# A graph layer with a mixture of experts on one core: a reworked first stage, and 30 transposes of the identity on TensorE among its first transposes

## The reference

```python
# _layernorm subtracts the mean and divides by sqrt(var + 1e-5)
def gnn(H, W, bias, edge_row, edge_col, edge_val):      # H (1024, 512), 16384 edges
    HW = H @ W
    msgs = edge_val[:, None] * HW[edge_col]
    out = segment_sum(msgs, edge_row, num_segments=1024)
    return relu(out + bias)

x = x + gnn(_layernorm(x), W, bias, src, dst, edge_weight)
x = x + ffn(_layernorm(x))
# ffn: each of 1024 rows goes to the best 2 of 64 experts (512 -> 256 -> 512, silu gate),
# and to one shared expert (512 -> 32 -> 512); the experts' weights are 100 MB in float32
```

## Time and profile before

| what | value |
|---|---|
| median of 3 runs | 459.57 us (458.48 to 460.67) |
| the profiled execution | 458.82 us |
| its span in the trace | 457.1 us |
| granted TensorE clock, mean | 0.932 |
| PE busy | 391.7 us (86%) |
| VectorE (DVE) busy | 207.7 us (45%) |
| ScalarE (ACT) busy | 166.1 us (36%) |
| GpSimd (POOL) busy | 154.9 us (34%) |
| HBM read, written | 121.22 MB, 13.39 MB |

### The profile page before, as it was taken

How to read it: one execution, slowest core, us unless ns; L and a number is a source line. 1 busy time by engine, 2 the same in 40 slices (tenths; PEclk the granted TensorE clock), 3 DMA queues, 4 the chain that set the end, 5 groups by cost and what they waited for, 6 DMA issues and landing times.

```text
span 457.1 us, 6545 instructions
## 1 busy us (share of the span) xinstructions
PE 391.7 (86%) x1811; PEld 202.3 (44%) x1812; DVE 207.7 (45%) x685; ACT 166.1 (36%) x414; POOL 154.9 (34%) x262
## 2 busy tenths in 40 slices
PE   2699999999999987999999999986988979888600
PEld 1586767656565553344344443433434433343100
DVE  5889888216666586532333233313113123222036
ACT  9859999223223220233233323331213231131200
POOL 2575553014654657232333223323113122110000
PEclk9989999999999995899999999999889898898855
DMA  4999600100004545499999999999999999996068
GB/s 113 328 383 408 276 0 0 42 25 24 24 25 122 222 156 197 144 389 408 404 408 407 405 408 409 407 406 408 407 406 409 406 405 404 403 405 271 20 250 303
DMA packets 41779, 126.11 MB, mean 276 GB/s; under 512 B 7953, under 2 KB 8529, under 8 KB 41618
## 3 DMA queue, kind: packets, MB, share of 16 engines
q1 hardware_dynamic: 35954, 117.29, 66.3%
q0 software_dynamic: 5792, 8.43, 5.3%
HBM read 121.22 MB, written 13.39 MB: 294 GB/s over the span
## 4 chain that ended last, share of the span: by engine, by line
PE 81%; issue 5%; DMA 5%; DVE 3%; SPq 3%; POOL 1%; ACT 1%; ACTq 0%; DVEq 0%; POOLq 0%
PE bank L1295 29%; PE bank L1312 13%; PE bank L1168 12%; PE bank L1129 6%; PE bank L1136 6%; PE bank L1304 5%; PE bank L1288 4%; DMA w<-totals 2%; DMA X<-in_x_dram 2%; PE bank L1156 2%; PE bank L1187 1%; PE bank L1236 1%; PE bank L1177 1%; PE bank L1117 1%; SPq L398 1%
## 5 line engine op out<-in xcount | busy, mean ns | idle before, releaser
L1031 DVE SCALAR_TENSOR_TENSOR osl<-bank,b13T,osl 128x64 f32<-128x64 f32 x132 | 28.4, 277 | 171.5 <-ACT osl L675 171.5
L1295 PE MATMUL bank<-w,xhT 128*64 128x512 f32 x368 | 91.9, 645 | 14.7 <-issue 14.5
L668 ACT COPY xh<-bank 128x512 f32<-128x512 f32 x33 | 19.3, 585 | 149.0 <-PE bank L1295 149.0
L1168 PE MATMUL bank<-HW,AT 128*128 128x512 f32 x128 | 58.2, 592 | 0.0
L1295 PEld LDWEIGHTS bank<-w,xhT 128*64 128x64 f32 x368 | 28.6, 147 | 61.5 <-issue 60.1
L545 POOL DMA_INDIRECT totals<-osl,A x17 | 17.0, 1000 | 91.5 <-PE bank L1288 72.1
L1312 PE MATMUL bank<-w,osl 128*64 128x512 f32 x184 | 45.0, 608 | 3.2 <-DVE osl L1031 3.2
L545 POOL DMA_INDIRECT totals<-GW,A x16 | 16.0, 999 | 87.2 <-PE bank L1288 71.6
L587 ACT ACTIVATE osl<-iota,eT 128x128 f32<-128x128 f32 x128 | 39.0, 389 | 6.1 <-PE bank L1129 6.1
L541 POOL DMA_INDIRECT A<-nx_rows,A x33 | 34.4, 1041 | 10.5 <-issue 10.5
L1168 PEld LDWEIGHTS bank<-HW,AT 128*128 128x128 f32 x128 | 22.9, 191 | 21.0 <-issue 21.0
(11 more groups left out here) (208 smaller groups left out, 543.2 us busy)
## 6 DMA issues: line engine op xcount, KB each, us to landing
w<-in_L_ffn_W_dram SPq DMA_DIRECT2D x66, 1024.0 KB
A<-in_L_ffn_W_dram SPq DMA_DIRECT2D x15, 1024.0 KB
HW<-in_L_ffn_W_dram SPq DMA_DIRECT2D x10, 1024.0 KB
AT<-in_L_ffn_W_dram SPq DMA_DIRECT2D x5, 1024.0 KB
w<-totals SPq DMA_DIRECT2D x8, 512.0 KB, 7.5
w<-in_L_ffn_W_dram SPq DMA_DIRECT2D x6, 512.0 KB
X<-in_x_dram SPq DMA_DIRECT2D x4, 512.0 KB, 7.2
out_dram<-X SPq DMA_DIRECT2D x8, 256.0 KB, 5.7
```

The costliest lines, as they stand in the source:

```text
L1031: ins = v.scalar_tensor_tensor(hT[b][:, m, CAP * h:CAP * h + CAP], bank[4][:, (HC + m) * P + CAP * h:(HC + m) * P + CAP * h + CAP], b13T[: ...
L1168: ins = t.matmul(bank[4 + s % 2][:, :], AT[:, s % 2, k, :], HW[:, k, :], start=(k == 0), stop=(k == NB - 1))
L1295: ins = t.matmul(bank[2 + b][CAP * h:CAP * h + CAP, :], xe[b][:, c, CAP * h:CAP * h + CAP], up_w[v][:, h, :, c, :], start=(c == 0), stop=( ...
```

## The change

The first stage is written anew in several places, and 30 transposes of the identity matrix are added to TensorE's program.

- **Transfers.** The expert tables, `Ws` and `gs4` are issued from ScalarE's queue. SyncE's queue issues W right behind the first quarter of x, then the rest of x, then small vectors. The sentinel block lies in the last places of the weight ring, so the fourth pair of weights waits for its store to end.
- **Zeroing A.** Instead of ScalarE alone, VectorE zeroes 2600 columns, GpSimd 2800 and ScalarE 2920.
- **TensorE's order.** The first block of x is transposed and multiplied ahead of the wait for `edges_ready`, and every block's transposes come right behind the product of the block ahead of it. Line 1090's product comes behind the transposes of the tables and of block 0. In groups 1 to 7 the product and the next transposes come ahead of the four quads.
- **The copies of the transposes** out of PSUM go from ScalarE to VectorE (`transposed_rows`), but for block 0.
- **The statistics** of the rest of x, one piece of six blocks before, are three pieces of two blocks between quads; GpSimd's inverse deviations are split likewise.
- **M.** GpSimd makes two tiles of each odd quad (not in the first four quads), VectorE two there.
- **The table products** on GpSimd (`R`, `Wsb`) come ahead of its work on M.
- **The identity.** `keep_busy` transposes the identity into bank 7, which nothing reads: 14 times at the start, 6 times behind the edges' transposes, 6 times behind those of the tables, 4 times ahead of the first product.

```diff
-POOL_M = 1
+A_DVE, A_POOL = 2600, 5400
+def pool_tiles(q, first):
+    return 2 if q % 2 and not (first and q < 4) else 1
...
             sp.dma_start(X[:, 0:2, :], xv[:, 0:2, :]).then_inc(x_in[0], 16)
-            for to, a in ((raw_wg, Wg), (raw_g, gamma), (raw_b, beta)):
-                sp.dma_start(to, a.rearrange(v3, c=4)).then_inc(raw_in, 16)
...
+            sp.dma_start(GW[:, :, :], W.rearrange("(p c) n -> p c n", c=DC)).then_inc(gw_in, 16)
+            for i in range(1, 4):
+                sp.dma_start(X[:, 2 * i:2 * i + 2, :], xv[:, 2 * i:2 * i + 2, :]).then_inc(x_in[i], 16)
...
         def _(act):
             a = nc.scalar
-            a.memzero(A[:, :]).then_inc(a_chain, 4)
+            for to, of in ((raw_wg, Wg), (raw_g, gamma), (raw_b, beta)):
+                act.dma_start(to, of.rearrange(v3, c=4)).then_inc(raw_in, 16)
...
+            a.memzero(A[:, A_POOL:]).then_inc(a_chain, 1)
...
-            def sum_pair(r, j, with_x, first):
+            def transposed_rows(b, u):
+                dve.wait_ge(xhT_ps, b + 1)
+                if not isinstance(b, int) or b > 1:
+                    dve.wait_ge(hw_ps, b - 1)
+                v.tensor_copy(xhT[:, u, :, :].rearrange("p c n -> p (c n)"), bank[4 + u][:, :]).then_inc(xhT_ready, 1)
...
-                    if with_x and first and q == 1:
-                        mean_and_variance(range(2, NB))
...
+                    if with_x and q % 4 == 3 and not (last and u):
+                        transposed_rows(b + 1, 1 - u)
+                    if with_x and first and q in (3, 4, 6):
+                        c = {3: 2, 4: 4, 6: 6}[q]
+                        mean_and_variance(range(c, c + 2))
+                    if with_x and first and q in (5, 6):
+                        dve.wait_ge(rstd_ready, 2)
+                        standard_rows(q - 3, q - 5)
...
             pe.wait_ge(consts, 5)
+            def keep_busy(spare_bank, n):
+                for i in range(n):
+                    t.transpose(spare_bank[:, (i % DC) * P:(i % DC + 1) * P], ident[:, :], ident[:, :])
+            keep_busy(bank[7], 14)
             pe.wait_ge(edge_prepped, 1)
...
-            pe.wait_ge(base_ready, 1)
-            t.matmul(bank[1][:, 384:512], ones[0:1, :], neg_base, start=True, stop=True).then_inc(base_ps, 1)
+            keep_busy(bank[7], 6)
             pe.wait_ge(raw_in, 80)
...
+            keep_busy(bank[7], 6)
+            x_rows(0, 0)
+            pe.wait_ge(base_ready, 1)
+            t.matmul(bank[1][:, 384:512], ones[0:1, :], neg_base, start=True, stop=True).then_inc(base_ps, 1)
+
+            keep_busy(bank[7], 4)
+            x_product(0, 0)
+            x_rows(1, 1)
             pe.wait_ge(edges_ready, 1)
...
                 for u in range(2):
-                    if with_x:
-                        pe.wait_ge(xh_ready, j * 2 + u + 1)
...
+                    if with_x and not (first and u == 0):
+                        x_product(j * 2 + u, u)
+                        if not (last and u):
+                            x_rows(j * 2 + u + 1, 1 - u)
```

More of the change, by code:

```diff
@@ L451, in pair @@
                     for q in (2 * h, 2 * h + 1):
+                        if first and q in (5, 7):
+                            b = q - 3
+                            inverse_deviations(range(b, b + 2), b // 2 + 1)
                         if not first or q >= 4:
                             pool.wait_ge(quad_done[q % 2], half + (q // 2 - 1))
-                        elif q == 2:
-                            pool.wait_ge(raw_transposed, 2)
-                        hold(pool)
-                        for k in range(POOL_M):
+                            hold(pool)
+                        for k in range(pool_tiles(q, first)):
                             t = (q % 2) * QUAD + k
@@ L745, in mean_and_variance @@
                 ins.then_inc(stats_ready, 1)
+            v.memset(A[:, 0:A_DVE], 0.0).then_inc(a_chain, 2)
             dve.wait_ge(edges_in, 48)
@@ L832, in sum_pair @@
                         dve.wait_ge(raw_transposed, 2)
-                    for k in range(POOL_M, QUAD):
+                    for k in range(pool_tiles(q, with_x and first), QUAD):
                         t = j * 32 + (QUAD * q + k)
@@ L843, in sum_pair @@
                         sums(r, j - 1, q - BEHIND + 8)
+                    if with_x and q % 4 == 3 and not (last and u):
[6 more added lines that the diff above has]
+                        standard_rows(q - 3, q - 5)
+                    if with_x and not first and not last and q % 4 == 1:
+                        dve.wait_ge(rstd_ready, 4)
+                        dve.wait_ge(xhT_ps, b + 1)
+                        standard_rows(b + 2, u)
             def all_pairs(r, with_x):
                 sum_pair(r, 0, with_x, True)
-                with dve.Fori(1, NB // 2) as j:
+                with dve.Fori(1, NB // 2 - 1) as j:
                     sum_pair(r, j, with_x, False)
+                sum_pair(r, NB // 2 - 1, with_x, False, True)
                 for q in range(8 - BEHIND, 8):
@@ L1106, in _, with x_rows, x_product, pair @@
             ins.then_inc(raw_transposed, 1)
+            def x_rows(g, u):
+                pe.wait_ge(xh_ready, g + 1)
+                for c in range(DC):
+                    ins = t.transpose(bank[4 + u][:, c * P:(c + 1) * P], xh[:, u, c:c + DC * (P - 1) + 1:DC], ident[:, :])
+                ins.then_inc(xhT_ps, 1)
+            def x_product(g, u):
+                pe.wait_ge(gw_in, 16)
+                pe.wait_ge(xhT_ready, g + 1)
+                if not isinstance(g, int) or g > 1:
+                    pe.wait_ge(hw_ready, g - 1)
+                for c in range(DC):
+                    ins = t.matmul(bank[6 + u][:, :], xhT[:, u, c, :], GW[:, c, :], start=(c == 0), stop=(c == DC - 1))
+                ins.then_inc(hw_ps, 1)
+            keep_busy(bank[7], 6)
[5 more added lines that the diff above has]
+            x_rows(1, 1)
             pe.wait_ge(edges_ready, 1)
             R1 = pe.value_load(rounds_sb[0:1, 0:1], min_val=1, max_val=N // WIN)
-            def pair(r, j, with_x):
+            def pair(r, j, with_x, first=False, last=False):
                 half = pe.snap((r * (NB // 2) + j) * 4)
@@ L1131, in pair @@
                         ins.then_inc(quad_done[q % 2], 1)
-                    if with_x:
-                        pe.wait_ge(gw_in, 16)
-                        pe.wait_ge(xhT_ready, j * 2 + u + 1)
-                        for c in range(DC):
-                            ins = t.matmul(bank[6 + u][:, :], xhT[:, u, c, :], GW[:, c, :], start=(c == 0), stop=(c == DC - 1))
-                        ins.then_inc(hw_ps, 1)
-            with pe.Fori(0, NB // 2) as j:
+            pair(0, 0, True, first=True)
+            with pe.Fori(1, NB // 2 - 1) as j:
                 pair(0, j, True)
+            pair(0, NB // 2 - 1, True, last=True)
             with pe.If(R1 > 1):
```

96 lines of the change are left out of this document (47 added, 49 removed).

## The result

| | median, us | lowest to highest | runs |
|---|---|---|---|
| before | 458.74 | 457.39 to 460.67 | 8 |
| changed | 462.72 | 460.35 to 464.13 | 8 |

The ratio is 1.0076, 95% interval [1.0051, 1.0101]: slower by 4.0 us, where 456.4 was forecast. The profiled execution of the changed kernel took 460.35 us with a span of 458.6; it is the fastest of the eight.

What follows compares the result with a forecast made beforehand. TensorE was taken to bound the first stage, ScalarE right behind. Steps summed to A's transposes at 82.3 against 85.50, 3.2 us earlier: 458.82 - 3.2 = 455.6, 456.4 on the median; range 453.0 to 459.5.

Steps and rivals of the forecast that it cites:

- Rival 3: Slower: tables share transfer engines with W, and each microsecond landing beyond 8.1 costs one; up to 462.1 us; chance 0.07.
- Tables landed by 8.1: Expert tables at the start: five issues end at about 3.8, last lands at 7.2; 8.1 taken, when six identities end.
- Keys at 13.2: Final keys written by VectorE at about 13.2 us, where it was 11.54; this step loses 1.7 us.
- ScalarE's first one-hots at 10.0: ScalarE's nine issues, table load and 2.5 us zeroing put its first one-hots at about 10.0, before 9.12; hidden.
- First quads at 19.6: On TensorE, product 0 ends at 19.1, then transposes of 0.5, then quads 0 to 3 in 3.9.
- From the first quads to product 2, 14.7 us (19.6 to 34.3): VectorE bounds this part; PE waits for xh of block 2 until 28.1; product 2 starts at 34.3, before 42.33.
- Groups of 7.90: Groups 2 to 6 lose ScalarE's 0.5 us copies; between 7.80 and 7.95, 7.90 each, 39.5 together, to 73.8.
- From product 7 to A, 8.5 us (73.8 to 82.3): End of first stage: product 7 to 77.2, last four quads 3.9 to 81.1, bare memset and sum 1.2.
- The bare tail of 1.2: Behind the last quads, a memset, a sum and semaphores lie bare ahead of A's transposes: 1.2 us.
- Identities: 0.6 to 1 us of cost, and they don't raise the clock: Of the 30, 14 and 6 hidden, 6 and 4 on PE's path; some 0.6 to 1 us reaches the end.
- Rival 1: Identities raise the clock before product 0, which takes 3.44; about 2.2 us more gain, 454.2; chance 0.18.
- The stage behind 86 us moves along with the first: Weight loads from the fifth pair on start from TensorE steps, so first-stage savings shift all that follows equally.

Runs made afterwards that it cites:

- experiment 1: The changed kernel with GpSimd's eight table products behind its first pair and ScalarE's wait for them only ahead of its last pair: 460.60 us, ratio 1.0014.
- experiment 2: The changed kernel with the four small loads (Ws twice, gs, bs) issued by SyncE ahead of W: 455.25 us, ratio 0.991.
- kernel 9: The same program as experiment 2, measured once more in a later series: 456.42 us, ratio 0.9935.
- 5: The kernel of experiment 2 without the 30 identity transposes: 457.62 us, ratio 0.9981.
- kernel 8: The changed kernel with all nine small loads, tables too, issued by SyncE ahead of W and none by ScalarE: 456.64 us, ratio 0.9947.
- 11: kernel 8 without the 30 identity transposes: 457.95 us, ratio 0.9976.
- 3: The changed kernel without its 30 identity transposes, nothing else: 464.65 us, ratio 1.0108.
- experiment 12: The kernel before with nothing but the 30 identity transposes added, in four groups: 457.79 us, ratio 0.9972.
- kernel 4: The kernel of experiment 1 with 30 products of the identity by itself in place of its transposes: 460.53 us, ratio 1.0003.
- 6: The kernel of experiment 2 with 11 more products on TensorE just ahead of the transposes of A: 466.63 us, ratio 1.0183.
- 13: The changed kernel with the four small loads still on ScalarE but ahead of its five table loads: 463.33 us, ratio 1.0084.
- Experiment 7: The kernel of experiment 2 with the product for the key base ahead of TensorE's wait for the tables: 461.33 us, ratio 1.0053.
- 14: The changed kernel with the four small loads issued by SyncE directly behind W: 459.62 us, ratio 1.0022.
- 10: kernel 8 with the 30 identity transposes made into 30 products of the identity by itself: 457.89 us, ratio 0.9975.

## Why the prediction was wrong

Its sum was 3.2 us earlier at the transposes of A; measured, they are 4.7 later, and the medians differ by 4.0. Rival 3's upper bound of 462.1 lies near the 462.72 by luck: it has the tables 5.7 us late, and they were 2.9. In the reading of the earlier trace rows TensorE is at 9 tenths from the third slice on and not the second, and the transfers stand nearly still from the sixth; the sum does not use either. By its own steps:

- **The first 14 identities hidden to 4.9:** right (1.77 to 5.02; PE then waits for the edges until 6.37, since these too land later than before).
- **Tables landed by 8.1:** wrong, 11.03. The issues ended at 3.95, as summed, but the last table took 7.7 and not 3.4. The condition "if W beside them does not slow them" was written down and then priced at nothing. This was rival 3, given 0.07. Its sum runs one microsecond to one: 11.03 is 2.9 late, near its break-even of 11.3. So, by that sum, the tables account for about the predicted gain, and not for the loss. T2, the tables as the whole cause, falls with experiment 1, where they are as late and A comes 2.9 us earlier.
- **Keys at 13.2:** 16.45, that is 3.25 later: 2.9 from the tables, and 0.35 in the transposes behind them.
- **ScalarE's first one-hots at 10.0:** 12.05. Its nine issues did not take 0.6 each; the sixth to the ninth took 0.92, 1.18, 1.21 and 0.79. In experiment 2 they were back at 10.32; what the delay cost by itself was not tried. The first quads had these one-hots ready at 17.17, so it was not what held them.
- **First quads at 19.6: the step that failed.** They started at 26.04. The sum went from keys to VectorE's tiles and from product 0 to the quads, and never asked what GpSimd's tile waits for. The diff moves eight products and a wait for four loads ahead of it, and puts those loads last on ScalarE's queue. They ran from 20.94 to 24.7, and GpSimd began the tile at 25.09. This term is missing from the sum and from every rival. Experiment 1 takes the products and both waits for them out of the way, with every load as late as before: first quads 22.49, A 2.9 us earlier. Experiment 2 takes out the late landing of bs and, with it, 1.45 us of the tables': first quads 21.52, A 4.6 earlier. Even then A starts 3.3 us behind the 82.3 of the sum (85.58): 1.8 of it are there at the keys (15.00), 2.4 at product 2 (36.70).
- **Product 0 of 5.0 us, first passes 0.86 apart:** 5.25, right.
- **From the first quads to product 2, 14.7 us (19.6 to 34.3):** 15.3 (26.04 to 41.31), right in size; VectorE's chain and the wait for xh of block 2 showed as soon as the quads were no longer late (2.12 us in experiments 1 and 2). The wait for GpSimd cost the clock too: the granted clock was 0.50 from 27.4 to 30.6 us, and quads 0 to 3 took 2.78 and 2.90 a pair, against 1.95 in experiment 2.
- **Groups of 7.90:** 7.53 and 8.55 for the first two (41.31, 48.84, 57.39), and product 7 starts at about 81.05 (80.88 in PE's timeline, which has product 2 at 41.14, 0.17 ahead of the chain), so five groups of 7.95: as before, and 0.05 each over the sum. The extra was to go with ScalarE's copies; the chain of this stretch is VectorE's, which has taken them over. Whether VectorE sets the groups was not tried.
- **From product 7 to A, 8.5 us (73.8 to 82.3):** 9.2, as the last four quads took 4.5 instead of 3.9. With 6.4 at the first quads, 0.6 and 0.25 this 0.7 makes the 7.9 us between 82.3 and 90.21.
- **The bare tail of 1.2:** 1.20 idle ahead of the transposes of A. Right.
- **Identities: 0.6 to 1 us of cost, and they don't raise the clock:** the runs lean the other way. In three pairs the kernel with them is the faster: 0.9935 against 0.9981 (kernels 9 and 5), 0.9947 against 0.9976 (8, 11), 1.0076 against 1.0108 (changed, 3), and 0.9972 on the kernel before alone (12). The intervals of each pair overlap, the three pairs are each from different series, and kernel 9 is odd for a reason of its own (below), so it isn't shown; but all four have one sign, 0.3% to 0.5%. Rival 1's mechanism is seen in some executions (last section). The rule of the Trainium skill (TensorE: Matmul & The Clock Gate, Part 4: PE-mode transpose) that I had let stand, that the full clock does not engage for transposes, doesn't agree with these traces: in experiment 12 nothing but transposes ran ahead of edge transposes of 0.27, where they took 0.42 without.
- **"The stage behind 86 us moves along with the first":** in one execution, to the last pair of products, yes (before 418.78, changed 423.48, +4.7). Behind that an execution gives or takes 3 us of its own, and the profiled one of the changed kernel gave back 3.2.

The medians of the 15 kernels follow the place of A roughly, up to 2.5 us off, but for kernel 2 (measured again as 9) and kernel 4, whose profiled execution took 464.17 us. Single profiles scatter as well: what kernels 2, 9 and 6 have in common up to the transposes of A ended at 85.58, 86.30 and 84.94. So a difference of about 1.4 us or less in the second column is not shown by itself.

| kernel | A at, us | against before | median against before (ratio - 1, of 459) |
|---|---|---|---|
| 6 | 94.75 | +9.2 | +8.4 |
| 13 | 91.86 | +6.4 | +3.9 |
| 3 | 90.65 | +5.2 | +5.0 |
| changed | 90.21 | +4.7 | +3.5 |
| 4 | 90.18 | +4.7 | +0.1 |
| 7 | 87.81 | +2.3 | +2.4 |
| 1 | 87.31 | +1.8 | +0.6 |
| 14 | 87.06 | +1.6 | +1.0 |
| 9, 2 | 86.30, 85.58 | +0.8, +0.1 | -3.0, -4.1 |
| 5 | 84.95 | -0.6 | -0.9 |
| 12 | 84.75 | -0.8 | -1.3 |
| 11 | 84.37 | -1.1 | -1.1 |
| 10 | 83.47 | -2.0 | -1.1 |
| 8 | 81.92 | -3.6 | -2.4 |

**What stays open.** Kernel 2, measured twice, is about 4 us faster than its first stage explains. So its gain is not the one that was forecast. In its first profile the part from A to the end took 367.9 us, against 371.6 in that of before; in its second 369.9, in the middle of what the 16 profiles spread over (367.9 to 372.2). So the program's two series agree, its two profiles don't, and I have no cause for it. Kernel 2 is the best that was found: 0.991 and 0.9935 of before, and, from the medians, some 1.5% under the changed kernel, which was not timed beside it.

## What to carry to other kernels

When a diff moves an instruction ahead of others on its engine, write down for every engine, GpSimd too, what it waits for and who stands behind it; the first product of a stage starts with the last of its inputs, and the sum must name all of them. A load that is small isn't early for that reason, and a queue of its own doesn't make it so: issue what gates the start ahead of the first megabyte on the queue that carries it, and put work that waits for the rest behind the first tiles, as experiments 2 and 1 do. Experiment 7 is the same error on TensorE, made by me after I had seen it on GpSimd.

## What the runs showed of the hardware

- **Two queues take turns by packets, not by bytes.** The profile's rows of the queues from 9 to 15 us of the changed kernel (packets, MB, share of 16 engines; q1 is SyncE's, q10 ScalarE's, as it is missing where ScalarE issues nothing):

```profile
q1 hardware_dynamic: 1226, 1.96, 91.4%
q10 hardware_dynamic: 1223, 0.17, 18.1%
```

As many packets each, but ScalarE's had 0.14 KB on average and SyncE's 1.6, so ScalarE's queue moved a twelfth of the bytes; kernels 1 (1136 and 1137) and 3 (1260 and 1256) show the same. The Trainium skill (DMA: Bandwidth & Descriptors, Queues, rings and completion order) has each transfer engine take turns between its queues, packet by packet, and in this stretch the trace agrees. bs, 2 KB, was not alone on its queue but stood behind eight loads, of which Ws comes in such small packets: it took 13.5 us to land there and 5.8 on SyncE's from nearly the same moment (issued at 7.38 and 6.73), and 2.2 on SyncE ahead of W, in kernel 8. From 5 to 9 us ScalarE's queue had 114 packets and SyncE's 291; whether it had run empty at times is not shown. The five tables took 2.9 to 7.0 in the changed kernel and 7.4 to 8.4 when issued 2.5 us later (13).
- **Not every issue takes the same time.** ScalarE's first five issues took 0.57 to 0.62 us each, the next four 0.79 to 1.21, while transfers were pending on both queues, and what stands behind them on that engine waits as well. Why they took longer was not tried.
- **Transposes can raise TensorE's clock, but not each time.** The third edge transpose took 0.27 us in the profiles of 3 kernels of the 10 with the 30 identity transposes (8, 12, 13), and 0.42 in the other seven; 0.27 in both with products of the identity (4, 10); 0.42 in all four without either (before, 3, 5, 11). The granted clock of the traces agrees: its first record is 1.00 from 4.7 to 6.0 us on in the five with 0.27; in two more with the transposes (1, 7) from 9.6 and 9.8; in the four without either not before 18.5. In five of these seven it did not last: it was 0.50 again from 11.6 to 13.2 us on (1, 4, 7, 12, 13), behind waits of 1.6 to 7.3 us; in 12 the six identities right behind its wait of 3.4 us still ran fast. With a wait of 0.9 us (8) or none (10) it stayed.
- **Ahead of the trace's first record of it, the row of the granted clock says 1.00 whatever the clock.** For 6.4 to 8.2 us it says 1.00 for kernel 2 and for kernel 8, though the third edge transpose lasts 0.42 in one and 0.27 in the other, and 8 operations were counted against 13. The first record is at 19.5 us in kernel 2 and at 5.6 in kernel 8 (before: 19.3, behind its half-speed quads at 15.22). There the lengths of equal passes tell, not that row. Kernel 2's stretch and kernel 8's (us; length, PE busy; granted clock; DMA share, GB/s):

```profile
6.40:8.20 1.80, 1.80 (x8) 1.00 1.27 296
```
```profile
6.40:8.20 1.80, 1.80 (x13) 1.00 0.84 151
```

- **The last pair of products takes 3.65 us (5 of the 16 profiles) or about 5.3 (11)** behind an idle of 1.7 to 2.1 us in all. The granted clock was 0.50 from 418.8 to 422.0 in the kernel before, and 1.00 from 423.5 to 427.0 in the changed one. The chain of the kernel before, and of the changed one:

```profile
416.80 1.98 issue
418.78 5.25 PE bank L1295 x16
```
```profile
421.54 1.93 issue
423.48 3.65 PE bank L1350 x16
```

It is one reason why one execution of this kernel tells less than its median, and why the place of an event in the first stage is the better witness of a change there.
